# First attention of a four-part sequence: the causal mask moves from TensorE's pass A to VectorE's row maximum

## What is computed

```
# part 1: causal attention, 16 heads of 8
q, v, k = split(h @ Wqvk)
scores = einsum('bshi,bthi->bsth', q, k) + where(t > s, -inf, 0)
weights = softmax(scores / sqrt(128), over t);  out = (weights @ v) @ Wo
# part 2: 8 experts of 352, the best two of each token
# part 3: attention without a mask, 16 query heads, 4 key heads;
#         q and k are multiplied by a rope factor that depends on the position
# part 4: hidden 512 with a sine transform, relu, second matrix, bias
```

## Time and profile before

| | |
|---|---|
| median of 3 runs | 1833.55 us (1832.67 to 1840.69) |
| span of the profiled execution | 1849.6 us, 30683 instructions |
| first attention, from its first maximum to the last L853 | about 62 to 637 us |
| experts and second projection | about 640 to 1000 us |
| second attention | about 1000 to 1750 us |
| PE busy over the span | 92% |
| DVE busy over the span | 74% |
| ACT busy over the span | 61% |

### The profile page before, as it was taken

How to read it: one execution, slowest core, us unless ns; L and a number is a source line. 1 busy time by engine, 2 the same in 40 slices (tenths; PEclk the granted TensorE clock), 3 DMA queues, 4 the chain that set the end, 5 groups by cost and what they waited for, 6 DMA issues and landing times.

```text
span 1849.6 us, 30683 instructions
## 1 busy us (share of the span) xinstructions
PE 1706.0 (92%) x10574; PEld 723.9 (39%) x10574; DVE 1363.6 (74%) x2397; ACT 1130.4 (61%) x2364; POOL 251.8 (14%) x337
## 2 busy tenths in 40 slices
PE   5599999999998897999789999999999999999888
PEld 3244444444444364665322222222232222222266
DVE  7678788788888164454798888888888888885287
ACT  4157676666665642333324777777777777777776
POOL 5100000002222236354610000000000000000010
PEclk9589999999999998999657999999999999999999
DMA  9445454423310011131331111111111111000000
GB/s 256 140 114 131 119 153 109 59 31 51 59 23 17 26 38 53 46 89 41 102 80 18 18 18 18 18 18 18 18 18 18 18 17 15 6 1 1 1 18 29
DMA packets 97576, 93.73 MB, mean 51 GB/s; under 512 B 47214, under 2 KB 75507, under 8 KB 95376
## 3 DMA queue, kind: packets, MB, share of 16 engines
q1 hardware_dynamic: 87360, 53.70, 16.7%
q0 software_dynamic: 9920, 37.87, 5.8%
q10 hardware_dynamic: 144, 0.20, 0.1%
HBM read 48.03 MB, written 40.86 MB: 48 GB/s over the span
## 4 chain that ended last, share of the span: by engine, by line
PE 73%; DVE 13%; issue 4%; ACT 4%; DMA 3%; POOL 2%; another core or an unknown queue 1%; SPq 0%; DVEq 0%; POOLq 0%; ACTq 0%
PE ps L866 20%; PE ps L850 18%; PE ps L817 16%; DVE rowmax L1505 8%; PE ps L1047 2%; PE ps L1027 2%; PE ps L1019 2%; PE ps L882 2%; PE ps L1037 2%; PE ps L1115 1%; PE ps L853 1%; ACT probs L1246 1%; PE ps L820 1%; DMA V<-v 1%; PE ps L757 1%
## 5 line engine op out<-in xcount | busy, mean ns | idle before, releaser
L1505 DVE TENSOR_REDUCE rowmax<-ps 128x1 f32<-128x1024 f32 (+7 forms) x1024 | 977.2, 988 | 217.4 <-PE ps L817 120.7
L1246 ACT ACTIVATE probs<-ps 128x512 f32<-128x512 f32 (+3 forms) x1280 | 604.8, 539 | 262.6 <-PE ps L853 125.6
L817 PE MATMUL ps<-K,Q 72*128 72x512 bf16 (+3 forms) x1792 | 534.3, 376 | 37.4 <-DVE rowmax L1505 14.5
L850 PE MATMUL ps<-Q,K 75*128 75x512 bf16 (+3 forms) x1792 | 555.2, 361 | 13.8 <-ACT probs L1246 6.7
L850 PEld LDWEIGHTS ps<-Q,K 75*128 75x128 bf16 x1792 | 167.7, 98 | 373.8 <-ACT probs L1246 130.0
L866 PE MATMUL ps<-probs,V 128*9 128x512 f32 (+3 forms) x2560 | 285.7, 536 | 0.0
L817 PEld LDWEIGHTS ps<-K,Q 72*128 72x128 bf16 x1792 | 158.9, 99 | 278.1 <-DVE rowmax L1505 86.8
L1246 ACT ACTIVATE wu<-ps 128x512 f32<-128x512 f32 x256 | 142.3, 611 | 41.9 <-PE ps L850 41.1
L1246 ACT ACTIVATE wg<-ps 128x512 f32<-128x512 f32 x256 | 144.0, 602 | 28.8 <-PE ps L850 27.0
L1756 DVE TENSOR_TENSOR Q<-ps,Q 128x352 f32<-128x352 f32 x78 | 40.9, 524 | 113.2 <-ACT Q L1293 76.6
L618 POOL TENSOR_SCALAR rtmp<-mv 128x4 f32<-128x4 f32 x8 | 1.6, 199 | 863.8 <-DVE mv L1421 863.8
(11 more groups left out here) (237 smaller groups left out, 1523.1 us busy)
## 6 DMA issues: line engine op xcount, KB each, us to landing
dispatch<-wg POOLq DMA_DIRECT2D x16, 1170.0 KB, 7.7
Q<-q_parts SPq DMA_DIRECT2D x288, 64.0 KB
K<-k_parts SPq DMA_DIRECT2D x144, 64.0 KB
Q<-dispatch SPq DMA_DIRECT2D x78, 65.0 KB
q_parts<-Q POOLq DMA_DIRECT2D x12, 384.0 KB, 4.0
probs<-returned SPq DMA_DIRECT2D x8, 512.0 KB, 3.9
V<-v SPq DMA_DIRECT2D x16, 144.0 KB
K<-k_parts SPq DMA_DIRECT2D x144, 16.0 KB
```

The costliest lines, as they stand in the source:

```text
L817: last = pe.matmul(buf[:, c:e], Q[0:CROSS, slot, j, i * P:(i + 1) * P], K[0:CROSS, slot, kj, c:e], start=True, stop=not diag)
L850: last = pe.matmul(ps[:, bank, c:HALF], K[0:KROWS, q, kj, t * P:(t + 1) * P], Q[0:KROWS, q, j, h * HALF + c:(h + 1) * HALF], start=True, s ...
L1246: act.activation(prob(l, 4 * m + j)[:, c:HALF], ps[:, B_BANKS[(4 * m + j) % 3], c:HALF], ACT.Exp, scale=SCALE).then_inc(sl["exp_done"], 1)
L1505: dve.tensor_reduce(rowmax[:, par, 8 * j + i:8 * j + i + 1], score_a(i % 2)[:, 0:hd.keys(i)], AX, ALU.max).then_inc(sl["max_done"], 1)
```

## The change

Pass A loses its mask product. `row_max` of the first attention becomes a `tensor_tensor_reduce`: it adds a row of zeros that ends in the 128 columns of mask to the scores, writes the sum (bf16) to one of two scratch buffers, and takes the maximum of it. The second attention keeps its `tensor_reduce`. The zeros and the mask lie in the first half of `ropeT` and the scratch buffers in its second half and in `tokens`; the rope table is therefore loaded during the experts. GpSimd zeroes 1024 columns in place of 128. A new instruction waits for the maximum two places earlier, whose scratch buffer it reuses. The string of the first attention changes.

```diff
-    "bbbaabbabapababbabbbappabbababbabbabapbcabbabpbabababtppbnababbabbabbappababbababbabbpbmasbbbappcatn",
+    "bbbaabababbbaapabbbabppabbababbabbabapbcbababpbabbtpnababbabapabbbababpbabbapababbabbpbmasbbbappactn",
...
+        ahead = ropeT[:, 0:S // 2].bitcast(BF16)
+        causal = ahead[:, S - P:S]
+        masked = (ropeT[:, S // 2:S].bitcast(BF16), tokens[:, :, :].rearrange("p t d -> p (t d)").bitcast(BF16))
...
-            (b2r[:, :], b2.rearrange("(a d) -> a d", a=1).broadcast_to([P, D])), (ropeT[:, :], rope),
+            (b2r[:, :], b2.rearrange("(a d) -> a d", a=1).broadcast_to([P, D])),
...
+                            if g == 0 and t == BACK[0]:
+                                sp.wait_ge(s[0]["attn_done"], 2 * NQ + AT_ONE)
+                                sp.dma_start(ropeT[:, :], rope).then_inc(rope_in, 16)
...
-            own.done(pool.memset(causal[:, :], 0.0))
+            own.done(pool.memset(ahead[:, :], 0.0))
...
-                        diag = hd.causal and e == w
                         last = pe.matmul(buf[:, c:e], Q[0:CROSS, slot, j, i * P:(i + 1) * P],
-                                         K[0:CROSS, slot, kj, c:e], start=True, stop=not diag)
-                        if diag:
-                            last = pe.matmul(buf[:, w - P:w], identb[:, :], causal[:, :],
-                                             start=False, stop=True)
+                                         K[0:CROSS, slot, kj, c:e], start=True, stop=True)
...
+                        dve.wait_ge(rope_in, 16)
...
+                    if hd.causal:
+                        if n >= 2:
+                            dve.wait_ge(sl["max_done"], n - 1)
+                        dve.tensor_tensor_reduce(masked[n % 2][:, 0:w], score_a(i % 2)[:, 0:w], ahead[:, S - w:S], 1.0, LOWEST,
+                                                 ALU.add, ALU.max, highest).then_inc(sl["max_done"], 1)
+                    else:
+                        dve.tensor_reduce(highest, score_a(i % 2)[:, 0:w], AX, ALU.max).then_inc(sl["max_done"], 1)
```

More of the change, by code:

```diff
@@ L50 @@
 MASKED = -1e30
+LOWEST = -3e38
 NQ = B * 4
@@ L281, in build @@
         identb = sb("identb", [P, P], BF16)
-        causal = sb("causal", [P, P], BF16)
         wqvk = rows_flat[:, 0:3 * D]
@@ L300, in build @@
         b2r = sb("b2r", [P, D])
+        tokens = sb("tokens", [P, GT, D])
         ropeT = sb("ropeT", [P, S])
+        ahead = ropeT[:, 0:S // 2].bitcast(BF16)
+        causal = ahead[:, S - P:S]
+        masked = (ropeT[:, S // 2:S].bitcast(BF16), tokens[:, :, :].rearrange("p t d -> p (t d)").bitcast(BF16))
         BT = T // B
@@ L315, in build @@
         power = sb("power", [P, GT])
-        tokens = sb("tokens", [P, GT, D])
         tokens2 = rows_flat[:, 0:GW].rearrange("p (t d) -> p t d", t=GT)
@@ L405, in build @@
         x_in = [sem(f"x_in{b}") for b in range(B)]
-        wqvk_in, w_in = sem("wqvk_in"), sem("w_in")
+        wqvk_in, w_in, rope_in = sem("wqvk_in"), sem("w_in"), sem("rope_in")
         consts, k_ones = sem("consts"), sem("k_ones")
@@ L1504, in row_max @@
                     dve.wait_ge(sl["scores"], n + 1)
-                    dve.tensor_reduce(rowmax[:, par, 8 * j + i:8 * j + i + 1], score_a(i % 2)[:, 0:hd.keys(i)],
-                                      AX, ALU.max).then_inc(sl["max_done"], 1)
+                    w, highest = hd.keys(i), rowmax[:, par, 8 * j + i:8 * j + i + 1]
+                    if hd.causal:
[5 more added lines that the diff above has]
+                        dve.tensor_reduce(highest, score_a(i % 2)[:, 0:w], AX, ALU.max).then_inc(sl["max_done"], 1)
                 def negmax_split(g, par):
```

## The result

The changed kernel takes 1820.74 us, the median of five runs (1819.66 to 1825.34), against 1833.55; the ratio of the runs is 0.9934, with a 95% interval of 0.991 to 0.9958: 12 us faster, between 7.7 and 16.5. The forecast was 1831 with an own range of 1821 to 1841, and the stated range of all rivals was 1807 to 1855.

A forecast was written before the change was run, and what follows sets the result against it. PE bounds plain groups; PE and VectorE take turns in routed ones. Terms -5.6 + 3 + 0.5 + 0.2 - 0.5 = -2.4 us on the median 1833.55 gave 1831 us, own range 1821 to 1841, all rivals 1807 to 1855.

The forecast's parts named there:

- Bounds of the groups: First attention: groups without routing are bound by PE; in groups with routing PE and VectorE take turns.
- The price of the read-out: VectorE's second instruction, reading the maximum out, costs 0.065 us each, 2.1 us a group; bounds 0 to 0.21.
- Rival 2: VectorE becomes the bound because the read-out also exposes the sum's drain, 0.14 us each; 1850 named; chance 0.25.
- The product's 0.057 us: Each mask product removed from pass A saves PE 0.057 us, 1.8 us a group, 29 us in all where PE bounds.
- The eight groups without routing: First attention up to 340 us: each plain group 0.7 us shorter, 30.3 us, -5.6 us in all.
- The routed groups: Seven first-attention groups up to about 602 us: each 37.6 us, +0.4, so +3 us in all.
- Prelude: Forty maxima with nothing beside them at half clock: +0.1 us per eight, +0.5 us in all.
- The string: The new order separates two products with V, recovering about 0.9 us of VectorE's idle in plain groups, 0.6 in routed.
- The head and the rope: Program start: GpSimd's longer zeroing costs +0.2 us; taking the rope load away there gives -0.5 us.
- Rival 1: PE's gain in full: the new string feeds VectorE evenly, all 15 groups lose 1.8 us; 1811 us; chance 0.30.
- Rival 3: TensorE's clock falls within groups as PE has less work, about 3 us per fall, five falls; 1846 us; chance 0.05.
- The clause on the profiled execution: The profiled execution lies 16 us above the median, in stretches the terms do not depend on, so they apply to the median.

The follow-up runs named there:

- e6: Changed kernel, but VectorE takes first-attention maxima (group 2 on, tiles of 256 columns and more) over only the upper half of the columns; one run, 1795.4 us.
- e4: Kernel before, with old string and plain reduce, but no mask product in pass A; ratio 0.9945 to the kernel before.
- e3: Changed kernel with the old string, VectorE adding the mask and PE still adding its product in pass A; ratio 1.0029 to the kernel before.
- e5: Changed kernel, but ScalarE takes exponentials of only half the columns in first-attention pass B from group 1 on; one run, 1811.8 us.
- e9: The changed kernel itself, unaltered, timed and profiled a second time; ratio 0.9928 to the kernel before.
- e1: Changed kernel with the string of the kernel before, so only the mask's move and later rope load; ratio 0.9953 to the kernel before.
- e7: Changed kernel with the 32 mask products of pass B left out as well; one run, 1824.9 us.

## Why the prediction was right or wrong

**Bounds of the groups: right.** Plain groups PE's, routed ones shared, said from the earlier trace rows. For the plain ones e6 shows it, where VectorE's relief gives nothing. For the routed ones e6 and e4 show it together: VectorE's relief gives 2.6 to 2.8 us, PE's 0.7. One reading on the way was off: between the waits at 388 and 405 us lie 15 maxima, not some 20.

**The price of the read-out: a step that failed.** I took 0.065 us, nearest to the row of small instructions without waits. Measured: from sum to sum 0.750 us over 640 columns, and 0.883 over 768, 8 to 9 ns over the reduce's; e3 prices it at nothing in a plain group and about 0.01 us in a routed one. I had 0 as the lower end and set it aside. The row of small instructions gives the distance of two that follow each other; the read-out lies in the end of the sum's own record, its drain, 1.215 - 1.14 = 0.075 us, which the prediction used for the opposite, to make the second rival dearer. A cover was in my rows and I did not ask what could lie under it. Rival 2 falls with it. The Trainium skill (VectorE: DVE Perf Modes, section on two Vector instructions with no wait between them) had the read-out as a second instruction that is not held when the start quadrants stay the same; the trace agrees, 511 of 512 read-outs starting inside their sum. The fixed 75 ns of the Trainium skill's Vector Engine (DVE) Microarchitecture Reference, section Measured stream behaviour on trn2, fits the sums (0.750 us at 640 columns is 0.667 and 0.083) and not the read-out.

**The product's 0.057 us: right at its place, not in the group.** The plain group was to lose 1.8 us on PE, of which VectorE's idle time would take back 1.1. It lost 0.93, close to the 0.7 forecast, for another reason: e4, with VectorE untouched, has the same 30.1. The step that failed is that "PE alone would allow 29.2 us", with every other distance in its queue left as it was. The 32 places gained 1.55 us, but other matmuls then waited 0.61 us more (e4); e5 shows that exponentials hold 0.4 us of a group, and ScalarE is a neighbour that the prediction's sum does not have. Two errors, a read-out too dear and a queue without its other waits, made a nearly right sum for the plain group.

**Terms, forecast and measured.** The eight groups without routing -5.6 us, measured -7.9 (250.4 to 242.6), and -7.0 in e9. The routed groups +3 in all; the six before the last window measured -3.3 in e9, and -1.8 in the changed kernel's first profile, where the clock fell once. Here the sign was wrong: VectorE's new instructions cost 0.3 us in a group where 2.1 were expected, and PE had less to do. Prelude +0.5; from the first maximum to the first splitting it was 27.6 us and became 26.1, and e1, e3 and e4 had 26.1, 27.7 and 26.0: -1.5, from the products at half clock in the chain between two maxima, of which I had counted a part and added a read-out that costs next to nothing. Together -11 to -12 before the last window, whose two profiles give +2.9 and 0, against a measured -12 (7.7 to 16.5). That the terms meet the time so closely is in part luck, since the last window and the rest of the program each move by some us from execution to execution. The total forecast, -2.4 us, was too small by a factor of five; its range was wide enough to hold the result.

**The string: wrong.** I gave it 0.9 us of VectorE's idle time in a plain group. It took that much from the longest wait and the other waits took it back. e1 against the changed kernel: nothing. In a routed group 0.6 was given; measured 0.1 to 0.25, once 0.6.

**The head and the rope: not settled**, -0.3 forecast, too small to be seen: the first maximum comes between 59.9 and 62.3 us in these programs, with no pattern that follows the rope. PE's first product moved from 11.67 to 12.04 us, 0.37 for the 0.2 that I had from the longer zeroing.

**Rival 1** (all of PE's gain) stood at 1811, as far from the result as the forecast. It was right that VectorE would not hold the plain groups. Its mechanism did not come: VectorE's idle time in a plain group was to fall to 2.1 us and is 5.0, and the full 1.8 us a group were not to be had even without any work added to VectorE (e4). **Rival 3** (the clock) did not decide the result, but it is there: one fall of 1.5 us in one of two profiles of the changed kernel, perhaps a part of the last window's 3 us, and falls in every full routed group with 32 more products gone (e7).

**The clause on the profiled execution** ("16 us above the median, in stretches that the terms do not depend on") held: most of what that execution lost, it lost in the experts.

## What to carry to other kernels

Before pricing an added instruction by what such instructions cost in a row, look at the drain of the one before it: a read-out that follows a long operation may fit in it whole. A removed product gives back its distance to the next start where it stood, here 0.058 us, but the queue as a whole can keep less of it, here 0.029 us, when it waits for other engines at other places. One experiment that removes the product and leaves everything else tells the price before the work of moving it is done, and laying its trace beside the old one, matmul by matmul, tells where the rest went. Where two versions differ in one window only, profile each twice: the window here moved by 3 us between executions of one program.

## What the runs showed of the hardware that was not expected

The read-out of this sum's maximum starts about 75 ns before the end of the sum's record (511 of 512), and the next VectorE instruction starts at the same moment in over half of the cases (282). Sum and read-out together take 8 to 10 ns more than a plain reduce of the same width.

A small bf16 product is followed by another bf16 one after 0.058 to 0.060 us when nothing is waited for (rows of e4 above), and by an fp32 one with nine columns of weights after 0.15, in all 81 cases of the kernel before between 104 and 560 us. PE, kernel before:

```profile
307.83 0.22 PE L820 MATMUL ps<-causal,identb 128*128 128x128 bf16 x1
307.98 0.61 PE L866 MATMUL ps<-probs,V 128*9 128x512 f32 x3
```

Taking the bf16 product away still gained 0.058 us there: the matmul in front of it then takes the longer distance to the fp32 one.

The granted clock fell in groups where PE is recorded as busy 33.86 of 37.66 us (e7), and stayed at its upper level in groups of 33.34 of 36.49 us (the changed kernel). The busy time of a group alone does not tell whether the clock falls in it.
